# Normalising an attention output in its transposed form, with transfers that spread values and sums to dense rows

## The chip, the cores and the metric

One NeuronCore of a Trainium2 chip runs the whole kernel. The metric is device time in microseconds (us), the median of several executions.

## The reference, cut to what matters

Input x is (16, 256, 256): 16 sequences of 256 tokens with 256 features, all in float32. For each sequence:

```python
h   = sln(x, cond)                     # LayerNorm, then a gamma and a beta that depend on cond
qkv = (h @ Wqkv.T + bqkv)              # split into 16 heads of 16 features
att = softmax(q @ k.T) / 16            # per head, 256 x 256
out = (att @ v)                        # per head, back to (256, 256)
h1  = out @ Wp.T + bp + x
y   = sln(h1, cond) + h1
```

## The kernel before, in words

The kernel is one software pipeline over the 16 sequences (B = 16). In step b, sequence b has its scores exponentiated and weighed with V, sequence b+1 has its row maxima taken, b+2 its Q and K projected, b+3 its x normalised and transposed, b-1 its attention output projected, and b-2 its residual and second LayerNorm. A step has 16 slots, one for each head h. No scheduler places anything: the order of every engine is written out by hand, slot by slot, in a `step(b)` function per engine, and semaphores tie the engines together.

In each slot TensorE (`step`, L1253) does two matmuls of scores (`scores`, into `st_ps`, which ScalarE exponentiates, L602) and two of scores for the maxima (`scores_max`, L1010, into `sa_ps`, which VectorE reduces, `maximum`, L692). `sa_ps` has two banks, so `scores_max` of slot h waits for the reduce of slot h-2 (L1017). The projections are spread over the slots in quarters: `Q_SLOTS`, `K_SLOTS`, `V_SLOTS`, `P_SLOTS` (L45). All matmuls of one source line L976 (`mm`).

The part around the change is the way from P.V to the output projection, by two groups g of eight heads:

- `weigh` (L1038): P.V, transposed. Four heads at a time lie in 32-partition bands of `pv_ps[g]`; 16 partitions hold values, the other 16 the softmax sum, since V is stored beside 16 columns of ones (`v_st`, memset L475, written by ScalarE at L540). Group 0 runs in slot 10 of step b, group 1 in slot 2 of step b+1 (`PV_SLOTS`).
- `evict_out` (L544): ScalarE copies the 128x512 bank to `oT` in slots 12 (`S_O0`) and 3 (`S_O1`).
- `out_by_token` (L1058): TensorE turns it back with four 128x128 transposes (L1065), in slots 14 and 6.
- `normalise` (L704): VectorE takes reciprocals of 128x16 sums (L711, slots 15 and 7) and multiplies 128x256 values into `att` (L715, slots 15 and 8).
- `turn_att` (L1141): four more transposes (L1146) in slot 10.
- ScalarE makes the rounded high part `aT_h` (L575, slot 11), VectorE the low part `aT_l` (`low_att`, L773, L777, slot 11), and TensorE multiplies with `Wp` in slots 12 to 15 (`project_out`, L1002).

VectorE's order is the dictionary `between` (L857). A key (h, 0) stands ahead of the reduce of slot h, (h, 1) behind it. The statistics of x (`norm1`, L732: bn_stats L739, bn_aggr L745, variance L749) stand for sequence b+3 in slots 4 and 5. `residual` (L780) stands in slots 3, 4, 9 and 11, `low_qk` (L719, L727) in 5 and 7.

GpSimd (`step`, L417) does `rstd` and `norm_x` in slot 5, `add_beta` in 6, `maxima` (two small transfers of the row maxima, L368) in 3 and 11, `low_h` in 12. SyncE's queue issues in order (`step`, L308): eight transfers for group 1 of sequence b+1 (`stack`, L297), the load of x for b+4 (L314), eight for group 0 of b+2, then `gb` (L328) and the output (L332). The last sequence has an order of its own (`last_step` L1189, `finish` L1224, and VectorE's list from L930).

Of the kernel before, what the change touches and what calls it, by code (L numbers as in the profile page):

```python
# [45 lines left out]
S_MT1, S_AT, S_MT0, S_XT = 1, 10, 9, 10  # L46
# [8 lines left out]
S_OT1, S_OT0 = 6, 14  # L55


def cond_block(nc, x, condT, vectors, WgT, WbT, WqkvT, WpT, bp, out):
    gb_dram = nc.dram_tensor("gb_rows", (B, 2 * D), F32, kind="Internal").ap()
    with ExitStack() as ctx:  # L60
# [55 lines left out]
        rec = sb("rec", [P, 2, TT, HH, 1])  # L116
        att = sb("att", [P, TT, D])
# [86 lines left out]
        o_done = sem("o_done")  # L204
        rec_ready = sem("rec_ready")
        att_ready = sem("att_ready")
        attT_done = sem("attT_done")
# [5 lines left out]
        aT0_done = sem("aT0_done")  # L213
# [59 lines left out]
        def _(sp):  # L273
# [81 lines left out]
        def _(pool):  # L355
# [54 lines left out]

            def low_full(a, t, ready):
# [5 lines left out]
            def step(b):  # L417
                for h in range(H):
# [56 lines left out]
            pool.memset(v_st[:, :, :, :, HD:VC].rearrange("p a t h d -> p (a t h) d"), D ** 0.5).then_inc(v_ones_ready, 1)  # L475
# [10 lines left out]
            add_beta(B - 3)  # L486
            add_beta(B - 2)
# [8 lines left out]
        def _(act):  # L496
# [39 lines left out]
            def high_v(a, ps):  # L536
# [3 lines left out]
                nc.scalar.activation(v_st[:, par(a), :, :, 0:HD],  # L540
# [3 lines left out]
            def evict_out(a, g):  # L544
# [4 lines left out]
                wait(act, o_done, 2 * (a - 1) + g + 1)  # L549
# [123 lines left out]
            wait(act, o_done, 2 * B - 2)  # L673
# [3 lines left out]
            act.wait_ge(aT0_done, 1)  # L677
            wait(act, proj_done, B - 1)
            nc.scalar.activation(aT_h[:, 0, :], sa_ps[1][:, 0:N], ACT.Copy).then_inc(aTth_ready, 1)
# [4 lines left out]
        def _(dve):  # L684
# [19 lines left out]
            def normalise(a, g, stage):  # L704
# [27 lines left out]
            def norm1(a, stage):  # L732
# [8 lines left out]
                if stage == 1:  # L741
                    wait(dve, v_step, 3 * a + 1)
                    dve.memset(pause[:], 0.0)
# [28 lines left out]

            def low_att(a):  # L773
                if not has(a):
                    return
                wait(dve, aTh_ready, 1 * a + 1)
                dve.tensor_tensor(aT_l[:].rearrange("p k n -> p (k n)"), pv_ps[1][:],  # L777
                                  aT_h[:].rearrange("p k n -> p (k n)"), ALU.subtract).then_inc(aTl_ready, 1)
# [42 lines left out]
            def last_out(a, g):  # L821

                wait(dve, pv_done, 2 * a + g + 1)
                wait(dve, o_done, 2 * (a - 1) + g + 1)
                dve.tensor_copy(oT[:, g, :], pv_ps[g][:]).then_inc(oT_ready, 1)

            def last_high_att(a):

                wait(dve, attT_done, 1 * a + 1)
                wait(dve, proj_done, 1 * (a - 1) + 1)  # L830
                dve.tensor_copy(aT_h[:].rearrange("p k n -> p (k n)"), pv_ps[1][:]).then_inc(aTh_ready, 1)

            def low_att_half(k):

                bank = (sa_ps[1], pv_ps[1])[k]
                wait(dve, aTth_ready, k + 1)
                dve.tensor_tensor(aT_l[:, k, :], bank[:, 0:N], aT_h[:, k, :], ALU.subtract).then_inc(aTtl_ready, 1)

            def normalise_half(c):
# [14 lines left out]
            def step(b):  # L854
# [13 lines left out]
                    (11, 0): [lambda: low_max(b + 1, 0), lambda: low_att(b - 1), lambda: residual(b - 2, 5)],  # L868
                    (15, 0): [lambda: normalise(b, 0, 0)],
# [514 lines left out]
```

## Time and profile before

| what | value |
|---|---|
| median of 3 runs | 347.57 us (345.4 to 347.86) |
| the profiled execution's own time | 345.56 us |
| its span, first to last instruction | 343.8 us |
| TensorE busy, of the span | 97% |
| VectorE busy | 87% |
| ScalarE busy | 71% |
| GpSimd busy | 46% |
| granted TensorE clock, mean | 1.000 of full speed |

Busy shares say how long an engine had an instruction under way. TensorE's matmuls are pipelined and their ends modelled, so its 97% says that it is hardly ever without work, not that it runs at its peak. Durations of neighbouring VectorE instructions overlap by some 0.08 us, so what one costs in a full queue is the distance from its start to the start of the next.

### The profile page before, as it was taken

The page shows a single profiled execution, that of the slowest core. Times are in us where ns is not written, and L with a number is a line of the kernel's source. Part 1 is how long each engine was busy: PE and PEld are TensorE (multiplying, and loading weights), DVE is VectorE, ACT ScalarE, POOL GpSimd, SP SyncE. Part 2 cuts the span into 40 slices and gives each one's busy share as a digit, 9 for nine tenths or more (in the row PEclk, how much of TensorE's full clock was granted, in tenths as well). Part 3 has the DMA queues.
Part 4 walks back from the last instruction along what each step waited for, and adds up shares of the span by engine and source line. Part 5 has one row for each costly group of instructions (what it writes and reads, how often), then busy time and mean ns, then how long its engine had stood idle before and what let it go on. Part 6 is the DMA issues. An engine that isn't in the chain of part 4 may idle for free.

```text
span 343.8 us, 8981 instructions
## 1 busy us (share of the span) xinstructions
PE 332.5 (97%) x3173; PEld 286.8 (83%) x3173; DVE 298.3 (87%) x728; ACT 242.8 (71%) x476; POOL 159.1 (46%) x187
## 2 busy tenths in 40 slices
PE   8888999999999999999999999999999999999993
PEld 4677879888888988888888988888898988888773
DVE  4888978799898989899898989989898988999684
ACT  7664876868676786868686876868687786766740
POOL 5765544437164545527264644617254643224330
PEclk9999999999999999999999999999999999999999
DMA  7396445456555454555545454655556354652021
GB/s 242 126 218 186 124 115 140 129 155 157 170 141 156 134 152 135 173 156 170 142 125 169 134 155 134 184 142 160 161 135 157 98 157 123 182 146 67 16 61 61
DMA packets 47705, 48.87 MB, mean 142 GB/s; under 512 B 6287, under 2 KB 41374, under 8 KB 47662
## 3 DMA queue, kind: packets, MB, share of 16 engines
q1 hardware_dynamic: 44494, 46.74, 49.2%
q10 hardware_dynamic: 1184, 1.07, 1.2%
q0 software_dynamic: 1984, 0.51, 0.8%
q8 instruction: 25, 0.41, 0.5%
q14 instruction: 18, 0.15, 0.1%
HBM read 9.99 MB, written 4.23 MB: 41 GB/s over the span
## 4 chain that ended last, share of the span: by engine, by line
PE 87%; DVE 5%; DMA 3%; ACT 1%; issue 1%; ACTq 1%; SPq 0%; DVEq 0%
PE m L976 24%; PE st L976 19%; PE sa L976 18%; PE pv L976 17%; PE pv L1065 4%; DVE mx L692 3%; PE pv L1146 2%; PE m L1105 2%; DMA wqkv<-WqkvT_dram 2%; DMA kst<-qk_l 1%; PE pv L1079 1%; PE m L1079 1%; ACT p L602 0%; DVE qk_l L727 0%; ACTq L625 0%
## 5 line engine op out<-in xcount | busy, mean ns | idle before, releaser
L692 DVE TENSOR_REDUCE mx<-sa 128x2 f32<-128x512 f32 x256 | 171.5, 684 | 28.4 <-PE sa L976 27.3
L602 ACT ACTIVATE p<-st 128x512 f32<-128x512 f32 x240 | 140.9, 598 | 37.5 <-PE st L976 33.2
L976 PE MATMUL sa<-kst,qst 126*128 126x256 f32 x512 | 105.6, 288 | 2.0 <-DMA kst<-qk_l 1.0
L976 PE MATMUL st<-qst,kst 128*128 128x256 f32 x496 | 104.1, 292 | 0.2
L976 PEld LDWEIGHTS st<-qst,kst 128*128 128x128 f32 x496 | 75.1, 188 | 13.8 <-issue 12.8
L976 PEld LDWEIGHTS sa<-kst,qst 126*128 126x128 f32 x512 | 78.6, 189 | 4.6 <-DVE mx L692 1.7
L368 POOL DMA_DIRECT2D qst<-m_h x31 | 17.6, 567 | 112.4 <-DVE m_l L701 112.4
L976 PE MATMUL pv<-p,v_st 128*32 128x256 f32 x1008 | 61.0, 382 | 0.0
L976 PEld LDWEIGHTS pv<-p,v_st 128*32 128x32 f32 x1008 | 29.5, 109 | 21.0 <-ACT p L602 1.5
L976 PE MATMUL m<-hT_h,wqkv_h 128*128 128x256 f32 x128 | 36.8, 300 | 1.3 <-ACT hT_h L616 0.7
L377 POOL TENSOR_SCALAR xn<-xa,mv,rstd 128x256 f32<-128x256 f32 x28 | 34.2, 1227 | 1.5
L976 PE MATMUL m<-hT_h,wqkv_l 128*128 128x256 f32 x128 | 34.4, 280 | 0.4 <-DVE wqkv_l L915 0.4
L976 PE MATMUL m<-hT_l,wqkv_h 128*128 128x256 f32 x128 | 34.3, 279 | 0.0
L429 POOL TENSOR_TENSOR rstd<-vare,minus_half 128x4 f32<-128x4 f32 (+1 forms) x15 | 14.2, 948 | 41.0 <-DVE vare L749 37.0
L550 ACT ACTIVATE oT<-pv 128x512 f32<-128x512 f32 x29 | 17.2, 595 | 21.6 <-PE pv L976 21.6
L727 DVE SCALAR_TENSOR_TENSOR qk_l<-m,vecs,qk_h 128x256 fp32r<-128x256 f32 x60 | 25.9, 474 | 0.5 <-ACT qk_h L522 0.5
L976 PEld LDWEIGHTS m<-hT_h,wqkv_h 128*128 128x128 f32 x128 | 23.5, 189 | 2.2 <-issue 1.1
L976 PEld LDWEIGHTS m<-hT_h,wqkv_l 128*128 128x128 f32 x128 | 23.6, 190 | 0.6 <-DVE wqkv_l L915 0.6
L976 PEld LDWEIGHTS m<-hT_l,wqkv_h 128*128 128x128 f32 x128 | 23.4, 188 | 0.0
L395 POOL TENSOR_TENSOR h1b<-h,gb 128x512 f32<-128x512 f32 x15 | 19.4, 1291 | 6.9 <-DVE h L788 6.9
L386 POOL TENSOR_TENSOR xa<-xa,bias_b 128x512 f32<-128x512 f32 x16 | 20.6, 1289 | 0.0
L409 POOL TENSOR_TENSOR hT_l<-hT,hT_h 128x512 fp32r<-128x512 f32 x14 | 18.0, 1288 | 5.2 <-ACT hT_h L503 5.2
(149 smaller groups left out, 566.2 us busy)
## 6 DMA issues: line engine op xcount, KB each, us to landing
qst<-qk_h SPq DMA_DIRECT2D x64, 128.0 KB, 2.4
qst<-qk_l SPq DMA_DIRECT2D x64, 128.0 KB, 2.5
kst<-qk_h SPq DMA_DIRECT2D x62, 128.0 KB, 2.5
kst<-qk_l SPq DMA_DIRECT2D x62, 128.0 KB, 2.8
xa<-x_dram SPq DMA_DIRECT2D x16, 256.0 KB, 3.0
gb<-gb_rows SPq DMA_DIRECT2D x16, 256.0 KB, 3.9
out_dram<-y SPq DMA_DIRECT2D x15, 256.0 KB, 3.4
wqkv<-WqkvT_dram SPq DMA_DIRECT2D x1, 512.0 KB, 5.6
```

Source lines behind the costliest of these rows:

```text
L368: pool.dma_start(raw(qst[MAX_ROW + r:MAX_ROW + 1 + r, p, g * HH:(g + 1) * HH, :]) .rearrange("a h (t n) -> a (h t) n", t=TT), raw(m[:, g, ...
L377: o = pool.tensor_scalar(xn[:, t, :], xbuf(a)[:, t, :], mv[:, t, 0:1], rstd[:, 0, t:t + 1], ALU.subtract, ALU.mult)
L386: pool.tensor_tensor(xbuf(a), xbuf(a), bias_b[:].rearrange("p (a n) -> p a n", a=1).broadcast_to([P, TT, D]), ALU.add).then_inc(xdb_ready, 1)
L395: pool.tensor_tensor(h1b[:], h1[:], gb[:, par(a), D:2 * D].rearrange("p (a n) -> p a n", a=1) .broadcast_to([P, TT, D]), ALU.add).then_inc ...
L409: pool.tensor_tensor(hT_l[:, par(a)], hT[:], hT_h[:, par(a)], ALU.subtract).then_inc(hTl_ready, 1)
L429: pool.tensor_tensor(rstd[:, which], vare[:, which], minus_half[:, which], ALU.pow).then_inc(rstd_ready, 1)
L550: nc.scalar.activation(oT[:, g, :], pv_ps[g][:], ACT.Copy).then_inc(oT_ready, 1)
L602: nc.scalar.activation(p32[:, h, :], st_ps[h % 2][:], ACT.Exp).then_inc(exp_done, 1)
L692: dve.tensor_reduce(mx[:, par(a), h // HH, (h % HH) * TT:(h % HH + 1) * TT], sa_ps[h % 2][:].rearrange("p (t n) -> p t n", t=TT), AX.X, AL ...
L727: o = dve.scalar_tensor_tensor(out=qk_l[:, par(a), t, g, :], in0=ps[:, g * N:(g + 1) * N], scalar=vecs[:, 4 + t, g:g + 1], in1=qk_h[:, par ...
L976: return nc.tensor.matmul(o, l, r, start=start, stop=stop)
L1065: o = nc.tensor.transpose(pv_ps[g][:, t * N + c * P:t * N + (c + 1) * P], oT[:, g, c * N + t * P:c * N + (t + 1) * P], ident[:])
```

## The change

V and the ones are interleaved, so that P.V leaves a value on each even partition and its sum on the odd one beside it. The 128x512 copy `oT` is then sent by two transfers of 128 KB per group: the 64 even partitions to `o_rows[:, g, :]` (128 partitions x 256) and the 64 odd ones to `o_sums[:, g, :]`. VectorE takes the reciprocal of `o_sums` (128x256, in place) and multiplies `o_rows` by it, in place. `o_rows` is now the transposed attention output, with its rows in an order that the host puts into `WpT` and the V bias. `out_by_token` and `turn_att` are gone. `aT_h` is made from `o_rows` in slot 10, `aT_l` by GpSimd instead of VectorE. The statistics of x move from slots 4 and 5 (for b+3) to 12 to 14 (for b+4).

```diff
-S_MT1, S_AT, S_MT0, S_XT = 1, 10, 9, 10
+S_MT1, S_AH, S_MT0, S_XT = 1, 10, 9, 10
-S_OT1, S_OT0 = 6, 14
...
+            def send_out(a, g):
+                if not has(a):
+                    return
+                sp.wait_ge(oT_ready, 2 * a + g + 1)
+                wait(sp, aTh_ready, 1 * a)
+                wait(sp, aTl_ready, 1 * a)
+                for n, dst in enumerate((o_rows, o_sums)):
+                    sp.dma_start(dst[:, g, :], oT[n:P:2, g, :]).then_inc(o_in[g], 16)
...
                     sp.dma_start(xbuf(b + 4), x_t[b + 4]).then_inc(x_in[(b + 4) % 4], 16)
+                send_out(b - 1, 1)
                 if has(b):
                     stack(b + 2, 0)
...
+                send_out(b, 0)
                 if has(b - 2):
                     wait(sp, y_ready, 1 * (b - 2) + 1)
...
+            def low_att(a):
+                wait(pool, aTh_ready, 1 * a + 1)
+                pool.tensor_tensor(aT_l[:], o_rows[:], aT_h[:], ALU.subtract).then_inc(aTl_ready, 1)
...
+                    if h == 10 and has(b - 1):
+                        low_att(b - 1)
                     if h == 11 and has(b):
                         maxima(b + 1, 0)
...
-                    if h == S_AT + 1 and has(b - 1):
-                        wait(act, attT_done, 1 * (b - 1) + 1)
+                    if h == S_AH and has(b - 1):
+                        wait(act, att_ready, 2 * (b - 1) + 2)
                         wait(act, proj_done, 1 * (b - 2) + 1)
-                        nc.scalar.activation(aT_h[:].rearrange("p k n -> p (k n)"), pv_ps[1][:],
-                                             ACT.Copy).then_inc(aTh_ready, 1)
+                        nc.scalar.activation(aT_h[:].rearrange("p k n -> p (k n)"),
+                                             o_rows[:].rearrange("p k n -> p (k n)"), ACT.Copy).then_inc(aTh_ready, 1)
...
-                sums = pv_ps[g][:].rearrange("p (t h d) -> p t h d", t=TT, h=HH)
                 if stage == 0:
-                    wait(dve, o_done, 2 * a + g + 1)
-                    dve.reciprocal(rec[:, g], sums[:, :, :, HD:HD + 1]).then_inc(rec_ready, 1)
+                    wait(dve, o_in[g], 32 * (a + 1))
+                    dve.reciprocal(o_sums[:, g, :], o_sums[:, g, :]).then_inc(rec_ready, 1)
                 if stage == 1:
                     wait(dve, rec_ready, 2 * a + g + 1)
-                    wait(dve, attT_done, 1 * (a - 1) + 1)
-                    dve.tensor_tensor(att[:, :, g * P:(g + 1) * P].rearrange("p t (h d) -> p t h d", h=HH),
-                                      sums[:, :, :, 0:HD], rec[:, g].broadcast_to([P, TT, HH, HD]),
+                    dve.tensor_tensor(o_rows[:, g, :], o_rows[:, g, :], o_sums[:, g, :],
                                       ALU.mult).then_inc(att_ready, 1)
...
-                    (2, 1): [lambda: low_max(b, 1)],
-                    (3, 0): [lambda: residual(b - 2, 0), lambda: residual(b - 2, 1)],
-                    (4, 0): [lambda: residual(b - 2, 2), lambda: norm1(b + 3, 0)],
-                    (4, 1): [lambda: residual(b - 2, 3), lambda: norm1(b + 3, 1)],
-                    (5, 0): [lambda: norm1(b + 3, 2)],
+                    (2, 1): [lambda: low_max(b, 1), lambda: normalise(b - 1, 0, 0)],
+                    (3, 0): [lambda: residual(b - 2, 0), lambda: normalise(b - 1, 0, 1), lambda: residual(b - 2, 1)],
+                    (4, 0): [lambda: residual(b - 2, 2)],
+                    (4, 1): [lambda: residual(b - 2, 3)],
...
-                    (11, 0): [lambda: low_max(b + 1, 0), lambda: low_att(b - 1), lambda: residual(b - 2, 5)],
-                    (15, 0): [lambda: normalise(b, 0, 0)],
-                    (15, 1): [lambda: normalise(b, 0, 1)],
+                    (12, 1): [lambda: norm1(b + 4, 0)],
+                    (13, 1): [lambda: norm1(b + 4, 1)],
+                    (14, 1): [lambda: norm1(b + 4, 2)],
+                    (11, 0): [lambda: low_max(b + 1, 0), lambda: residual(b - 2, 5)],
...
             low_max(B - 1, 1)
             for stage in (1, 2, 3):
                 residual(B - 3, stage)
+            normalise(B - 2, 0, 0)
+            normalise(B - 2, 0, 1)
             last_out(B - 2, 1)
+            residual(B - 3, 4)
             normalise(B - 2, 1, 0)
             normalise(B - 2, 1, 1)
             last_high_att(B - 2)
-            low_att(B - 2)
-            residual(B - 3, 4)
             last_out(B - 1, 0)
```

For the last sequence, the second group of heads keeps the old way (`normalise_half`, two transposes), with strides changed for the interleaved layout.

## Rows read from the trace of the kernel before

**Rows 1.** The page: busy time, and the chain that ended last

```profile
PE 332.5 (97%) x3173; PEld 286.8 (83%) x3173; DVE 298.3 (87%) x728; ACT 242.8 (71%) x476; POOL 159.1 (46%) x187
...
PE 87%; DVE 5%; DMA 3%; ACT 1%; issue 1%; ACTq 1%; SPq 0%; DVEq 0%
```

**Rows 2.** Busy time by engine in stretches of one step each

```profile
core 0: us, PE busy (x) PEld busy (x) DVE busy (x) ACT busy (x) POOL busy (x), PEclk, DMA share, GB/s
73.02:92.50 19.48, 19.48 (x197) 17.28 (x196) 17.82 (x45) 14.55 (x30) 9.38 (x10) 1.00 0.55 150
...
170.45:189.94 19.49, 19.49 (x196) 17.29 (x195) 17.84 (x44) 14.58 (x30) 9.38 (x10) 1.00 0.54 153
...
267.90:287.40 19.50, 19.50 (x197) 17.29 (x196) 17.85 (x44) 14.57 (x30) 9.36 (x10) 1.00 0.53 145
```

**Rows 3.** The chain in order of time, one step: start, us, what

```profile
173.62 0.44 PE pv L1065 x4
...
178.37 0.44 PE pv L1146 x4
178.80 1.86 PE pv L976 x32
183.51 0.44 PE pv L1065 x4
```

**Rows 4.** Timeline of VectorE in that step: start, us, instruction, [idle before]

```profile
174.87 0.25 DVE L711 RECIPROCAL rec<-pv 128x16 f32<-128x16 f32 x1
175.04 0.62 DVE L692 TENSOR_REDUCE mx<-sa 128x2 f32<-128x512 f32 x1
...
176.36 0.41 DVE L715 TENSOR_TENSOR att<-pv,rec 128x256 f32<-128x256 f32 x1
176.69 1.28 DVE L692 TENSOR_REDUCE mx<-sa 128x2 f32<-128x512 f32 x2
...
179.47 0.69 DVE L777 TENSOR_TENSOR aT_l<-pv,aT_h 128x512 fp32r<-128x512 f32 x1
180.08 0.87 DVE L816 SCALAR_TENSOR_TENSOR y<-y,rstd,h1b 128x256 f32<-128x256 f32 x2
181.38 1.98 DVE L692 TENSOR_REDUCE mx<-sa 128x2 f32<-128x512 f32 x3 [0.43 <-PE sa L976]
183.54 0.69 DVE L692 TENSOR_REDUCE mx<-sa 128x2 f32<-128x512 f32 x1 [0.18 <-PE sa L976]
...
187.40 0.69 DVE L692 TENSOR_REDUCE mx<-sa 128x2 f32<-128x512 f32 x1 [0.24 <-PE sa L976]
```

**Rows 5.** Groups of instructions with shapes kept apart: VectorE, small ones and multiplies

```profile
L711 DVE RECIPROCAL rec<-pv 128x16 f32<-128x16 f32 x31 | 7.7, 248 | 0.9 <-PE pv L1065 0.9
...
L843 DVE RECIPROCAL rec<-sa 128x8 f32<-128x8 f32 x1 | 0.2, 208 | 0.4 <-PE sa L1232 0.4
...
L843 DVE RECIPROCAL rec<-pv 128x8 f32<-128x8 f32 x1 | 0.2, 199 | 0.0
...
L893 DVE COPY vecs<-pv 128x14 f32<-128x14 f32 x1 | 0.2, 165 | 0.0
```

**Rows 6.** The same view: two float32 multiplies from PSUM, 256 and 128 columns

```profile
L715 DVE TENSOR_TENSOR att<-pv,rec 128x256 f32<-128x256 f32 x31 | 12.8, 414 | 0.1
...
L845 DVE TENSOR_TENSOR att<-pv,rec 128x128 f32<-128x128 f32 x1 | 0.3, 291 | 0.0
```

**Rows 7.** SyncE's queue in that step, and its line L297: us to landing

```profile
170.64 0.54 SPq L314 DMA_DIRECT2D xa<-x_dram  x1
174.69 1.17 SPq L297 DMA_DIRECT2D qst<-qk_h  x2
```

```profile
DMA to landing us min/median/max: 2.3/2.5/4.5
```

**Rows 8.** The last step: VectorE's timeline

```profile
322.36 0.69 DVE L825 COPY oT<-pv 128x512 f32<-128x512 f32 x1 [0.55 <-PE pv L976]
...
326.10 0.69 DVE L777 TENSOR_TENSOR aT_l<-pv,aT_h 128x512 fp32r<-128x512 f32 x1
```

**Rows 9.** The last step: the chain in order of time

```profile
328.59 1.41 PE m L976 x12
330.00 0.44 PE pv L1065 x4
```

**Rows 10.** Groups: one low part as GpSimd makes it

```profile
L409 POOL TENSOR_TENSOR hT_l<-hT,hT_h 128x512 fp32r<-128x512 f32 x14 | 18.0, 1288 | 5.2 <-ACT hT_h L503 5.2
```

**Rows 11.** Who waited for whom: us in total, times, longest us

```profile
PEld sa L976 <- DVE mx L692: 1.7, 5, 0.6
```

More of the change, by code:

```diff
@@ L115, in cond_block @@
         oT = sb("oT", [P, 2, 2 * N])
-        rec = sb("rec", [P, 2, TT, HH, 1])
-        att = sb("att", [P, TT, D])
+        rec = sb("rec", [P, TT, HH, 1])
+        o_rows = sb("o_rows", [P, 2, N])
+        o_sums, att = wg, wqkv[:, :, 0:D]
         aT_h = sb("aT_h", [P, KT, N], F32R)
@@ L486, in _ @@
             add_beta(B - 3)
+            low_att(B - 2)
             add_beta(B - 2)
@@ L548, in evict_out @@
                 wait(act, pv_done, 2 * a + g + 1)
-                wait(act, o_done, 2 * (a - 1) + g + 1)
+                wait(act, o_in[g], 32 * a)
                 nc.scalar.activation(oT[:, g, :], pv_ps[g][:], ACT.Copy).then_inc(oT_ready, 1)
@@ L672, in _ @@
             act.wait_ge(pvt_done, 1)
-            wait(act, o_done, 2 * B - 2)
+            wait(act, o_in[1], 32 * (B - 1))
             nc.scalar.activation(oT[:, 1, 0:N], pv_ps[1][:, 0:N], ACT.Copy).then_inc(oTt_ready, 1)
@@ L676, in _ @@
             nc.scalar.activation(oT[:, 1, N:2 * N], m0[:, 0:N], ACT.Copy).then_inc(oTt_ready, 1)
-            act.wait_ge(aT0_done, 1)
+            wait(act, att_ready, 2 * B - 1)
             wait(act, proj_done, B - 1)
-            nc.scalar.activation(aT_h[:, 0, :], sa_ps[1][:, 0:N], ACT.Copy).then_inc(aTth_ready, 1)
+            nc.scalar.activation(aT_h[:, 0, :], o_rows[:, 0, :], ACT.Copy).then_inc(aTth_ready, 1)
             act.wait_ge(aT1_done, 1)
@@ L742, in norm1 @@
                     wait(dve, v_step, 3 * a + 1)
+                    wait(dve, xn_ready, 1 * a)
                     dve.memset(pause[:], 0.0)
@@ L771, in low_h_direct @@
                 dve.tensor_tensor(hT_l[:, par(a)], hT[:], hT_h[:, par(a)], ALU.subtract).then_inc(hTl_ready, 1)
[L773 to L778, printed above, removed]
             def residual(a, stage):
@@ L823, in last_out @@
                 wait(dve, pv_done, 2 * a + g + 1)
-                wait(dve, o_done, 2 * (a - 1) + g + 1)
+                wait(dve, o_in[g], 32 * a)
                 dve.tensor_copy(oT[:, g, :], pv_ps[g][:]).then_inc(oT_ready, 1)
             def last_high_att(a):
-                wait(dve, attT_done, 1 * a + 1)
+                wait(dve, att_ready, 2 * a + 2)
                 wait(dve, proj_done, 1 * (a - 1) + 1)
-                dve.tensor_copy(aT_h[:].rearrange("p k n -> p (k n)"), pv_ps[1][:]).then_inc(aTh_ready, 1)
+                dve.tensor_copy(aT_h[:], o_rows[:]).then_inc(aTh_ready, 1)
             def low_att_half(k):
-                bank = (sa_ps[1], pv_ps[1])[k]
+                whole = (o_rows[:, 0, :], pv_ps[1][:, 0:N])[k]
                 wait(dve, aTth_ready, k + 1)
-                dve.tensor_tensor(aT_l[:, k, :], bank[:, 0:N], aT_h[:, k, :], ALU.subtract).then_inc(aTtl_ready, 1)
+                dve.tensor_tensor(aT_l[:, k, :], whole, aT_h[:, k, :], ALU.subtract).then_inc(aTtl_ready, 1)
             def normalise_half(c):
@@ L874, in step @@
                 if first(b + 1):
-                    for slot in ((4, 0), (4, 1), (5, 0), (5, 1), (7, 1), (11, 0)):
+                    for slot in ((4, 0), (4, 1), (5, 1), (7, 1), (11, 0)):
                         del between[slot]
@@ L942, in _ @@
             residual(B - 2, 0)
+            for stage in (1, 2, 3):
+                residual(B - 2, stage)
             normalise(B - 1, 0, 0)
             normalise(B - 1, 0, 1)
-            for stage in (1, 2, 3):
-                residual(B - 2, stage)
             normalise_half(0)
@@ L1041, in weigh @@
                 wait(pe, exp_done, 16 * b + HH * (g + 1))
-                wait(pe, att_ready, 2 * b + g - 1)
+                wait(pe, oT_ready, 2 * b + g - 1)
                 if g == 0:
@@ L1047, in weigh @@
                     pe.wait_ge((v_ones_ready, bias_ready)[g], 1)
-                if g == 1:
-                    wait(pe, aTl_ready, 1 * b)
                 for q in range(2):
@@ L1056, in weigh @@
                 o.then_inc(pv_done, 1)
-            def out_by_token(a, g):
-                if not has(a):
-                    return
-                wait(pe, oT_ready, 2 * a + g + 1)
-                for t in range(TT):
-                    for c in range(2):
-                        o = nc.tensor.transpose(pv_ps[g][:, t * N + c * P:t * N + (c + 1) * P],
-                                                oT[:, g, c * N + t * P:c * N + (t + 1) * P], ident[:])
-                o.then_inc(o_done, 1)
             def warm_up(n):
@@ L1139, in project_second @@
                 o.then_inc(q_done, 1)
-            def turn_att(a):
-                wait(pe, att_ready, 2 * a + 2)
-                for t in range(TT):
-                    for k in range(KT):
-                        o = nc.tensor.transpose(pv_ps[1][:, k * N + t * P:k * N + (t + 1) * P],
-                                                att[:, t, k * P:(k + 1) * P], ident[:])
-                o.then_inc(attT_done, 1)
             def last_scores(h):
@@ L1170, in last_weigh @@
                 if half == 0:
-                    wait(pe, aTl_ready, B - 1)
+                    wait(pe, oT_ready, 2 * (B - 2) + 2)
                 else:
@@ L1191, in last_step @@
                 last_scores(1)
-                wait(pe, att_ready, 2 * (B - 2) + 1)
+                wait(pe, oT_ready, 2 * (B - 2) + 1)
                 transpose_max(B - 1, 1, pv_ps[0])
@@ L1224, in finish @@
             def finish():
-                wait(pe, att_ready, 2 * B - 1)
-                for t in range(TT):
-                    o = nc.tensor.transpose(sa_ps[1][:, t * P:(t + 1) * P], att[:, t, 0:P], ident[:])
-                o.then_inc(aT0_done, 1)
+                wait(pe, oT_ready, 2 * B - 1)
                 for c, bank in ((0, sa_ps[0]), (1, pv_ps[0])):
@@ L1265, in step @@
                         turn_x(b + 3)
-                    if h == S_AT and has(b - 1):
-                        turn_att(b - 1)
                     for g in range(2):
@@ L1271, in step @@
                             weigh(a, g)
-                    if h == S_OT1:
-                        out_by_token(b - 1, 1)
-                    if h == S_OT0:
-                        out_by_token(b, 0)
                     if h == (0 if first(b) else S_MT1) and has(b):
-                        wait(pe, att_ready, 2 * (b - 1) + 1)
+                        wait(pe, oT_ready, 2 * (b - 1) + 1)
                         if first(b):
@@ L1364, in by_kind, with by_rows @@
                                w[:, :, 2].reshape((D,) + w.shape[3:])])
+    def by_rows(w):
+        return np.moveaxis(w.reshape((2, 2, HH // 2, HD) + w.shape[1:]), 1, 3).reshape(w.shape)
+    bqkv = by_kind(get("bqkv"))
     arrays = {
@@ L1374 @@
         "WqkvT": by_kind(get("Wqkv")).T,
-        "WpT": get("Wp").T, "bp": get("bp"),
+        "WpT": by_rows(get("Wp").T), "bp": get("bp"),
     }
```

19 lines of the change are left out of this document (7 added, 12 removed).

## The prediction

> **What bounds the kernel now.** I read the page's busy shares first, then its chain, then stretches of one step. TensorE is busy 97% of the span and has 87% of the chain [rows 1]. The stretches say it more sharply: from 73.02 to 287.40 us eleven steps in a row last 19.5 us each, and in each TensorE is busy for all of it, while VectorE is busy for 17.8 to 17.9 us (the first, one in the middle and the last of them: [rows 2]). So TensorE has no slack at all in the steady part, and VectorE has 19.49 - 17.84 = 1.65 us a step. That second number matters as much as the first, because the change takes work off the one and, as I will argue, puts work on the other. The clock stands at its upper level (2.4 GHz, a granted share of 1.00) in every step [rows 2].
>
> **TensorE: what goes.** Each step loses three blocks of four transposes, at 0.44 us each in the chain [rows 3]: 1.32 us. TensorE's own work per step falls to 19.49 - 1.32 = 18.17 us. Nothing is added on it.
>
> **VectorE: what goes.** Costs are taken from start to start [rows 4]. The low part of 128x512: 180.08 - 179.47 = 0.61 us. Two multiplies from PSUM at 176.69 - 176.36 = 0.33 us: 0.66. Two reciprocals of 128x16: 0.17 us in the full queue (175.04 - 174.87); the second stands alone and counts 0.25, its duration [rows 4, 5]. Together 1.69 us.
>
> **VectorE: what comes.** Two multiplies of 128x256, both operands now in SBUF. The one there is now, with an operand in PSUM, has a slope of (414 - 291) / 128 = 0.96 ns a column [rows 6], one column a cycle or so, and the new one has as many columns: 0.33 us each, 0.66 for the two.
>
> Two reciprocals of 128x256. This is the number on which the whole case turns, for the trace has none longer than 16 columns. What it has: 248 ns at 16 columns (31 of them) and 199 and 208 ns at 8 [rows 5]. The difference is 40 to 49 ns for 8 columns, 5.0 to 6.1 ns a column, where the multiply's slope would give 8 ns. A second way: a copy of 14 columns takes 165 ns [rows 5], of which some 150 are fixed if it goes at a column a nanosecond; then the reciprocals' rest is 98 ns for 16 and 49 to 58 for 8, 6 to 7 ns a column. A third: in the full queue one costs 0.17 us against about 0.07 us that a multiply costs over its columns (0.33 - 0.26), so 0.10 us for 16 columns. All three say some 6 ns a column. The strides can't explain that away wholly: the small reciprocals read one element in 32, but the multiply's 16-wide runs of the same bank pay nothing for the gaps. So I take 0.07 + 256 x 6.1 ns = 1.63 us in the queue for one. Bounds: below, 256 columns at the multiply's slope, 0.33 us, if the small ones' price is something fixed or due to single-element reads; above, 7 ns a column and 0.07, 1.86 us.
>
> VectorE then has 17.84 - 1.69 + 0.66 + 2 x 1.63 = 20.07 us of work in a step. That is more than the 19.49 us a step takes now, and more than TensorE's 18.17: the bound changes engine. VectorE still can't run without gaps, since a reduce waits for its scores. Before, it idles 0.43, 0.18 and 0.24 us ahead of bare slots [rows 4]; in slots 15, 0 and 1 of the new order it again has a reduce alone (0.61 us, half of a pair that lies without a gap, against a slot of over 0.8), and once more it catches up while TensorE weighs for 1.86 us in slot 10 [rows 3]. I add 0.6 us (0.2 for each of two or three slots and the rest there). A step of 20.65 us, then: 1.16 us more than now. TensorE stands still in it at slots 5, 9 and 10, where `scores_max` needs a bank that the reduce behind a long reciprocal or a `low_qk` has not yet freed.
>
> The Trainium skill ("VectorE: DVE Perf Modes", First, the fixed hardware budget) says that reciprocal runs on an iterative divide with a repeat count of 8. Read as eight cycles of 0.96 GHz a column, an estimate from that page, the long reciprocal takes 2.2 us and the step 21.8. By that rule the small ones would differ by 67 ns; the trace has 40 to 49 [rows 5] and doesn't agree in size, though it does in kind. Another page ("Vector Engine (DVE) Microarchitecture Reference", Measured stream behaviour on trn2) has built-in one-source operations at 1.0417 ns a column and 75 ns fixed: 0.34 us for the long one. The trace speaks against it by the same rows. Both are rivals below.
>
> **Moved and hidden parts.** The statistics of x cost VectorE the same in slots 12 to 14 as in 4 and 5; there they use slots that had little, which is why I add 0.6 us of idle and not the old 1.65. The x they need was loaded 8 slots earlier. ScalarE: the same copies, one read from SBUF and a slot earlier; it has 19.49 - 14.58 = 4.9 us of slack a step [rows 2], so nothing. Both interleaved strides (V and its ones) I take at nothing for the same cover. GpSimd: one more low part, 1.29 us [rows 10], on an engine busy 9.4 of 19.5 us [rows 2]; it stands ahead of the maxima's two transfers and `low_h`. `aT_h` can be ready in slot 10, before VectorE's row maxima of slot 11, so it is done by about the time the maxima can go: nothing; without that cover, a late first score in the next step, up to 1.3 us.
>
> **The transfers.** SyncE issues four more a step, each at 0.59 us (1.17 for two) [rows 7]. Those for group 1 stand behind eight stacks and the load of x, which is issued at 170.64; two more would be out by about 172.4 and land by 171.8 + 2.5 = 174.3, at worst 176.3 with 4.5 us [rows 7]. VectorE wants them at its slot 7, at 174.87 before [rows 4], and some 0.5 us later in the new step because a reciprocal and a multiply stand in slots 2 and 3. Behind that wait queues everything of VectorE, the reduce of slot 7 first, and so TensorE. Median landing gives 1 us of margin: nothing. The next stacks go at 174.69, after the two. Group 0's transfers have half a step. Bound above: 1 us a step.
>
> **The last step** has no reduces, but its order is a chain. The old one: copy at 322.36, transposes, reciprocal, multiply, turn, high part, low part ending at 326.79 [rows 8], projection from 328.59 [rows 9]. The new one puts a reciprocal and a multiply ahead of the copy (1.96, less 0.55 that VectorE idled there: copy at 323.8, done 324.5), then two issues and a landing (0.6 + 2.5: 327.6), reciprocal and multiply (1.96: 329.5), high part (0.7), low part on GpSimd (1.3): 331.5, against a projection at 328.59 now: 2.9 us late. Behind it another long reciprocal and multiply in place of short ones (1.96 for 0.6) stand on VectorE ahead of the last half, and 0.44 us of transposes at 330.00 go [rows 9]. I take +4 us, bounds 0 and 6.
>
> **The sum.** Sequences 0 to 13 pass the two normalisations inside 14 full steps: 14 x 1.16 = 16.2 us. Plus 4 at the end, less 0.44 for one block in step 0. From the profiled execution's 345.56 us: 365.3. The median of the runs shown is 347.57, 2.0 above; they spread by 2.5 us, so I give 365.
>
> **Rivals.**
> 1. *The long reciprocal streams at a column a cycle* (0.33 us). For: the trace has no long one, and the small ones read single elements. Against: the slope of rows 5. VectorE has 17.84 - 1.69 + 0.66 + 0.67 = 17.5 us, TensorE bounds at 18.2: 14 x 1.3 = 18 us saved, the end about even: 328. This is the case of the other side. The point from which it decides: VectorE's load plus idle equals 19.49 us at (19.49 - 0.6 - 16.81) / 2 = 1.04 us for one reciprocal, 3.8 ns a column. Below that the change is faster.
> 2. *The long reciprocal costs more than any reading of the short ones gives*, a column at twice the rows' lower slope of 4 or 5 ns, 2.2 us: 16.81 + 4.4 + 0.6 = 21.8 us a step, 14 x 2.3 + 5 = 37: 383. Against: rows 5 as said.
> 3. *The transfers come late*, because more of them share the engines or wait for the queue: 0.7 us a step on top, 10 us: 375. For: landings up to 4.5 us. Against: 1 us of margin.
> 4. *Something between* (3.5 to 4.5 ns a column): 342 to 354.
>
> **How the numbers follow.** Forecast 0.68, rival 1 0.14, rival 2 0.05, rival 3 0.07, rival 4 0.06. The forecast's own spread: 5.0 ns a column gives 1.35 us, a step of 20.1 and, with a shorter end, 357; 7 ns 1.86 us, 21.1 and 373. The range is 352 to 378: it leaves out rival 1 and 2. A measurement here can tell about 1% from no change. Faster by over 1%: rival 1 and a part of 4, 0.15; within 1%: 0.04; slower: 0.81.
>
> **What would show it.** Right: reciprocals of 128x256 at 1.5 to 1.8 us; VectorE over 95% busy in the steady part and first in the chain; TensorE waiting for the reduce (5 times and 1.7 us in all now [rows 11], then 2 us a step); steps near 20.6 us. Wrong: reciprocals of 0.4 us, with steps of 18.2 us and TensorE still without a gap; or VectorE idle ahead of its slot-7 reciprocal, released by a transfer.

## The result, and the profile after

The changed kernel takes 373.04 us (median of 4 runs, 372.62 to 376.89) against 347.54 us for the kernel before: a ratio of 1.077, 95% interval 1.069 to 1.086. Ratios, here and below, are of mean times, and leave out an execution more than 1.5% above the fastest of its kernel (one, in e3_apart). The forecast was 365 us, slower, with a range of 352 to 378. The profiled execution took 373.01 us, with a span of 371.2 us against 343.8.

The page of the changed kernel, busy shares and chain, the answer to [rows 1]:

```profile
PE 333.8 (90%) x2987; PEld 273.2 (74%) x2987; DVE 341.0 (92%) x713; ACT 245.6 (66%) x476; POOL 179.1 (48%) x202
...
PE 43%; DVE 38%; issue 13%; DMA 2%; ACT 1%; ACTq 1%; DVEq 0%; POOL 0%; SPq 0%
```

TensorE has 186 matmul records fewer, and yet the kernel is longer: its part of the chain went from 87% to 43%, and VectorE's from 5% to 38%. One step, in the busy times by stretch, the answer to [rows 2]:

```profile
core 0: us, PE busy (x) PEld busy (x) DVE busy (x) ACT busy (x) POOL busy (x), PEclk, DMA share, GB/s
160.54:181.45 20.91, 19.37 (x184) 16.23 (x183) 20.50 (x44) 14.74 (x30) 10.65 (x11) 1.00 0.59 169
181.45:202.36 20.91, 19.36 (x184) 16.20 (x183) 20.52 (x45) 14.77 (x30) 10.65 (x11) 1.00 0.57 163
```

A step lasts 20.91 us instead of 19.49 (forecast: 20.65). VectorE is busy for 20.5 of it (98%). Groups of the page that carry this, the first the answer to [rows 5]:

```profile
L728 DVE RECIPROCAL wg<-wg 128x256 f32<-128x256 f32 x31 | 53.7, 1733 | 1.9 <-DMA wg<-oT 1.9
...
L817 DVE SCALAR_TENSOR_TENSOR y<-h,mv,gb 128x256 f32<-128x256 f32 x30 | 24.5, 856 | 0.0
```

The long reciprocal takes 1733 ns (`o_sums` lies in the old tile `wg`). Against 248 ns at 16 columns that is 1485 / 240 = 6.2 ns a column, as the short ones had said. Behind it, VectorE's queue goes on 1.66 us after its start. The second row is one that I had not forecast; it comes back below.

The chain in order of time shows how a step hangs together (start, us, what):

```profile
184.24 0.67 DVE mx L710
184.90 1.66 DVE wg L728
...
188.21 0.69 DVE mx L710
188.90 0.04 issue
188.95 0.51 PE sa L986 x2
189.46 0.44 PE m L1102 x4
189.90 1.86 PE pv L986 x32
...
198.35 0.07 DVE mx L710
198.42 0.54 issue
198.96 0.27 DVE m_l L719
199.23 1.66 DVE wg L728
```

It isn't VectorE all round. From slot 2 (198.35) to the reduce of slot 8 (188.21 + 20.91 + 0.69 = 209.81) the step runs on VectorE, 11.5 us; there `scores_max` of slot 10 takes over, and up to the next slot 2 it runs on TensorE, 9.4 us. Who waited for whom confirms the place:

```profile
PEld sa L986 <- DVE mx L710: 29.0, 49, 1.4
```

That was 1.7 us in 5 times before [rows 11]; now it is some 2 us a step. In TensorE's timeline of one step these waits stand at slots 5, 9 and 10, the three that were forecast:

```profile
182.17 0.51 PE L986 MATMUL sa<-kst,qst 126*128 126x256 f32 x2 [0.43 <-DVE mx L710]
187.16 0.50 PE L986 MATMUL sa<-kst,qst 126*128 126x256 f32 x2 [0.37 <-DVE mx L710]
188.95 0.51 PE L986 MATMUL sa<-kst,qst 126*128 126x256 f32 x2 [0.42 <-DVE mx L710]
```

To see where the 27.4 us of span went, I take the start of the residual's bn_stats, once a step, as a mark. From the first to the twelfth mark the kernel before goes from 71.91 to 286.56 us and the changed one from 76.16 to 306.11: 15.3 us in 11 steps. Ahead of the first mark lie 4.25 us (two such steps make 2.8 of them; beside them the stretch from 30 to 40 us has a clock share of 0.83, against 1.00 before), in the step after the twelfth 1.6, in the last steps 6.2 (4.1 from mark 14 to 15 and 2.2 behind it).

**The end.** TensorE's timeline there (start, us, instruction, [idle before]), and the busy times of the stretch:

```profile
352.79 0.58 PE L986 MATMUL m<-wp_h,aT_h 128*128 128x256 f32 x1 [3.52 <-POOL aT_l L424]
353.17 0.41 PE L986 MATMUL m<-wp_h,aT_l 128*128 128x256 f32 x1
```

```profile
core 0: us, PE busy (x) PEld busy (x) DVE busy (x) ACT busy (x) POOL busy (x), PEclk, DMA share, GB/s
350.00:355.00 5.00, 2.21 (x10) 2.21 (x11) 3.35 (x6) 0.67 (x2) 1.27 (x1) 0.61 0.21 59
```

TensorE stood still for 3.52 us until GpSimd had the low part. Then the clock granted was the lower level, 1.2 GHz, for a part of the stretch (PEclk 0.61 over the whole), so that twelve matmuls that took 1.41 us before [rows 9] took 2.94. The wait I had forecast at 2.9 us; the 1.5 us of clock I had not.

### The profile page after: what moved, and what is told of

Same layout as the page of the kernel before. It is cut to its first block, busy times and chain, and to the rows that moved or that the text cites. A ratio compares the mean times of both kernels' runs of the same rounds, so it can differ in the third digit from the quotient of the medians.

```text
span 371.2 us, 8687 instructions
## 1 busy us (share of the span) xinstructions
PE 333.8 (90%) x2987; PEld 273.2 (74%) x2987; DVE 341.0 (92%) x713; ACT 245.6 (66%) x476; POOL 179.1 (48%) x202
## 4 chain that ended last, share of the span: by engine, by line
PE 43%; DVE 38%; issue 13%; DMA 2%; ACT 1%; ACTq 1%; DVEq 0%; POOL 0%; SPq 0%
DVE wg L728 14%; PE sa L986 13%; PE m L986 11%; PE st L986 9%; DVE mx L710 8%; PE pv L986 7%; DVE qk_l L742 5%; DVE stats L802 3%; DVE h L797 2%; PE m L1102 2%; DVE o_rows L731 1%; DVE m_l L719 1%; DMA kst<-qk_l 1%; DVE mv L808 1%; DVE y L817 1%
## 5 line engine op out<-in xcount | busy, mean ns | idle before, releaser
L710 DVE TENSOR_REDUCE mx<-sa 128x2 f32<-128x512 f32 x256 | 168.7, 672 | 14.1 <-PE sa L986 10.8
L986 PE MATMUL sa<-kst,qst 126*128 126x256 f32 x512 | 111.6, 300 | 19.9 <-DVE mx L710 18.7
L986 PEld LDWEIGHTS st<-qst,kst 128*128 128x128 f32 x496 | 76.5, 191 | 14.5 <-issue 12.4
L986 PE MATMUL pv<-p,v_st 128*32 128x256 f32 x1008 | 61.9, 386 | 0.0
L728 DVE RECIPROCAL wg<-wg 128x256 f32<-128x256 f32 x31 | 53.7, 1733 | 1.9 <-DMA wg<-oT 1.9
L986 PE MATMUL m<-hT_h,wqkv_h 128*128 128x256 f32 x128 | 36.0, 294 | 1.2 <-ACT hT_h L634 0.7
L424 POOL TENSOR_TENSOR aT_l<-o_rows,aT_h 128x512 fp32r<-128x512 f32 x15 | 19.4, 1292 | 31.9 <-ACT aT_h L593 25.6
L986 PEld LDWEIGHTS m<-hT_h,wqkv_h 128*128 128x128 f32 x128 | 23.7, 191 | 2.2 <-issue 2.2
L817 DVE SCALAR_TENSOR_TENSOR y<-h,mv,gb 128x256 f32<-128x256 f32 x30 | 24.5, 856 | 0.0
L986 PEld LDWEIGHTS m<-hT_l,wqkv_h 128*128 128x128 f32 x128 | 23.7, 190 | 0.0
```

The lines of the kernel that those rows point to most:

```text
L424: pool.tensor_tensor(aT_l[:], o_rows[:], aT_h[:], ALU.subtract).then_inc(aTl_ready, 1)
L710: dve.tensor_reduce(mx[:, par(a), h // HH, (h % HH) * TT:(h % HH + 1) * TT], sa_ps[h % 2][:].rearrange("p (t n) -> p t n", t=TT), AX.X, AL ...
L728: dve.reciprocal(o_sums[:, g, :], o_sums[:, g, :]).then_inc(rec_ready, 1)
L817: o = dve.scalar_tensor_tensor(out=y[:, par(a), t, :], in0=h1[:, t, :], scalar=mv2[:, t, 0:1], in1=gb[:, par(a), 0:D], op0=ALU.subtract, o ...
L986: return nc.tensor.matmul(o, l, r, start=start, stop=stop)
```

## The experiments

**b1_stats: the statistics of x alone.** In the kernel before:

```diff
+                    wait(dve, xn_ready, 1 * a)
...
-(4, 0): [lambda: residual(b - 2, 2), lambda: norm1(b + 3, 0)],
-(4, 1): [lambda: residual(b - 2, 3), lambda: norm1(b + 3, 1)],
-(5, 0): [lambda: norm1(b + 3, 2)],
+(4, 0): [lambda: residual(b - 2, 2)],
+(4, 1): [lambda: residual(b - 2, 3)],
+(12, 1): [lambda: norm1(b + 4, 0)],
+(13, 1): [lambda: norm1(b + 4, 1)],
+(14, 1): [lambda: norm1(b + 4, 2)],
```

> The kernel before with only the statistics of x moved to slots 12 to 14, for b+4. Theory: TensorE bounds, VectorE has 1.65 us a step to spare, so no change: within 0.3% of the kernel before. Rival (the move costs or saves by itself): over 0.5% either way.

Measured: 345.76 against 345.40 us, ratio 1.0005 (0.998 to 1.003). No change: the move costs nothing in the kernel before.

**b2_recips: the long reciprocals alone.** In the kernel before:

```diff
+            def spare(a, g):
+                if not has(a):
+                    return
+                dve.reciprocal(wb[:, g, :], wg[:, g, :])
...
-(2, 1): [lambda: low_max(b, 1)],
+(2, 1): [lambda: low_max(b, 1), lambda: spare(b - 1, 0)],
-(7, 0): [lambda: normalise(b - 1, 1, 0)],
+(7, 0): [lambda: normalise(b - 1, 1, 0), lambda: spare(b - 1, 1)],
```

> The kernel before with two reciprocals of 128x256 added to VectorE's list of each step, behind the low part of the maxima in slot 2 and behind the short reciprocal in slot 7; nobody reads what they write. Theory (the long reciprocals alone make VectorE the bound): 17.8 + 2 x 1.66 + some 0.4 us of idle, steps of 21.3 to 21.7 us, 371 to 378 us. Rival (the rest of the change, transfers and waits, makes most of the loss): steps under 20.3 us, below 360 us.

Measured: 381.58 us against 345.31, ratio 1.105 (1.100 to 1.111), steps of 22.33 us. The rival falls, and the time lies above the expected 371 to 378 us. Two instructions that nobody reads cost more than the whole change, which had taken other work off VectorE. The step is 0.6 us longer than the upper end of what load and idle gave. VectorE is busy for 20.96 us of it, near the load I had added up, and idle for 1.37 where I had taken some 0.4.

**e1_stream and e2_half: the reciprocal shortened.**

e1_stream inverts no sum, e2_half only half of the columns. First the edit of e1_stream, then that of e2_half:

```diff
-dve.reciprocal(o_sums[:, g, :], o_sums[:, g, :]).then_inc(rec_ready, 1)
+dve.tensor_tensor(o_sums[:, g, :], o_sums[:, g, :], o_sums[:, g, :],
+                  ALU.mult).then_inc(rec_ready, 1)
```

```diff
-dve.reciprocal(o_sums[:, g, :], o_sums[:, g, :]).then_inc(rec_ready, 1)
+dve.reciprocal(o_sums[:, g, 0:P], o_sums[:, g, 0:P]).then_inc(rec_ready, 1)
```

> The long reciprocal is replaced by a multiply of the same 128x256 tile with itself, in place (so the sums are not inverted; everything else stands). Theory (VectorE's load, made by the two long reciprocals, bounds the step): VectorE loses 2 x (1.66 - 0.33) = 2.7 us of work a step, TensorE bounds again without its transposes, steps of about 18.3 us, 330 us in all, some 5% faster than the kernel before. Rival (the transfers or the new waits bound it): still above 360 us.

> The long reciprocal runs over 128 of its 256 columns (half of the sums are not inverted). Theory: 6.4 ns a column, so 0.90 us instead of 1.73; VectorE's work falls by 2 x 0.83 us a step; steps of 19.2 to 19.4 us, 347 to 350 us: within 1% of the kernel before, which is near the break-even that I put at 1.04 us. Rival (a large fixed cost): a reciprocal of 1.2 us or more and over 355 us.

Measured: e2_half 359.38 us, ratio 1.040 (1.035 to 1.046), most steps 19.9 to 20.0 us (three of the first eleven 20.2 to 20.9; VectorE waited 8 times for a transfer, 6.7 us in all). e1_stream 349.14 us, ratio 1.008 (1.005 to 1.012), steps of 19.4 to 19.8 us. The reciprocal of 128 columns:

```profile
L728 DVE RECIPROCAL wg<-wg x31: 929/931/954, 53.9 to 345.0; 128x128 f32<-128x128 f32 x31
```

(min, median and max in ns.) Three lengths now: 248 ns at 16 columns, 931 at 128, 1733 at 256: 6.1 and 6.3 ns a column. That part of both expectations holds. The times don't: I had put break-even at 1.04 us for one reciprocal, and even a stand-in of 0.33 us only comes to about even. TensorE's work of some 18.2 us a step doesn't come through, so something else holds the step at 19.5. VectorE's timeline in e1_stream, ahead of slot 7:

```profile
195.32 0.43 DVE L728 TENSOR_TENSOR wg<-wg 128x256 f32<-128x256 f32 x1 [0.59 <-DMA wg<-oT]
```

There are nine such waits in the run, 5.7 us in all.

**e9_stream_xload: the transfer two thirds of a microsecond earlier.** In e1_stream, SyncE's queue:

```diff
+                send_out(b - 1, 1)
                 if has(b + 4) and has(b):
...
                     sp.dma_start(xbuf(b + 4), x_t[b + 4]).then_inc(x_in[(b + 4) % 4], 16)
-                send_out(b - 1, 1)
```

> e1_stream with the load of x issued behind the pair of transfers instead of ahead of it. Theory (with a short reciprocal, the transfer that slot 7 waits for holds the step): the pair goes out 0.55 us earlier, VectorE's wait of 0.6 us ahead of slot 7 goes, steps of 18.9 to 19.3 us instead of 19.5, 338 to 344 us. Rival (VectorE's order in slots 3 to 8 holds it): steps of 19.4 us or more.

Measured: 347.17 us, ratio 1.004 (1.001 to 1.008), beside e1_stream's 1.008: little. One of the seven waits in the steady steps is left (0.88 us; with three near the end 3.8 us in all), and the steps are still 19.5 us. What took the wait's place stands in the timelines of VectorE and of GpSimd:

```profile
195.50 0.87 DVE L743 SCALAR_TENSOR_TENSOR qk_l<-m,vecs,qk_h 128x256 fp32r<-128x256 f32 x2
196.28 1.33 DVE L732 TENSOR_TENSOR o_rows<-o_rows,wg 128x256 f32<-128x256 f32 x1
197.54 1.27 DVE L710 TENSOR_REDUCE mx<-sa 128x2 f32<-128x512 f32 x2
```

```profile
196.04 1.29 POOL L405 TENSOR_TENSOR h1b<-h,gb 128x512 f32<-128x512 f32 x1
```

The multiply takes 1.33 us where its median is 0.416. It starts 0.24 us after the start of a GpSimd instruction that ends at 197.33, and is done 0.28 us after that end. Both its operands lie in SBUF. The multiply that it replaces read PSUM and never took over 425 ns.

The same GpSimd instruction stands there in e1_stream. GpSimd, then VectorE:

```profile
196.10 1.29 POOL L405 TENSOR_TENSOR h1b<-h,gb 128x512 f32<-128x512 f32 x1
```

```profile
197.60 1.28 DVE L710 TENSOR_REDUCE mx<-sa 128x2 f32<-128x512 f32 x2
```

It ends at 197.39 there and at 197.33 here, and the reduces of slot 8, for which TensorE waits in both runs, start at 197.60 and 197.54. So the wait for the transfer was hidden behind the collision, and taking it away gained nothing here. No run has a short reciprocal with neither of the two and nothing in their place, so what the step would be then isn't shown.

**e3_apart: the same collision in the changed kernel.** There it hits y's first part, which is the odd row of the page above. The timelines of VectorE and GpSimd in the changed kernel:

```profile
189.41 1.73 DVE L817 SCALAR_TENSOR_TENSOR y<-h,mv,gb 128x256 f32<-128x256 f32 x2
191.07 0.68 DVE L710 TENSOR_REDUCE mx<-sa 128x2 f32<-128x512 f32 x1
```

```profile
189.19 1.28 POOL L424 TENSOR_TENSOR aT_l<-o_rows,aT_h 128x512 fp32r<-128x512 f32 x1 [1.18 <-ACT aT_h L593]
```

The pair took 0.87 us before. GpSimd's low part is what the change put there. The experiment moves the pair from behind the reduce of slot 9 to ahead of that of slot 11:

```diff
-(9, 1): [lambda: residual(b - 2, 4)],
-(11, 0): [lambda: low_max(b + 1, 0), lambda: residual(b - 2, 5)],
+(11, 0): [lambda: low_max(b + 1, 0), lambda: residual(b - 2, 4), lambda: residual(b - 2, 5)],
```

> VectorE's y = (h1 - mean) * gb (residual stage 4) moves from behind the reduce of slot 9 to ahead of that of slot 11, so that it no longer starts while GpSimd makes the attention's low part. Theory (the instruction with two SBUF inputs waits for the whole of the GpSimd instruction): its longest falls from 1.5 to under 0.6 us in the steady steps, a step gets 0.5 to 0.9 us shorter, 7 to 12 us in all: 361 to 366 us. Rival (the 1.5 us come from gb's transfer or from a semaphore): no change, 373 us.

VectorE's timeline in e3_apart:

```profile
190.27 0.27 DVE L719 SCALAR_TENSOR_TENSOR m_l<-m,m_h 16x128 fp32r<-16x128 f32 x1
190.47 0.86 DVE L817 SCALAR_TENSOR_TENSOR y<-h,mv,gb 128x256 f32<-128x256 f32 x2
...
192.64 1.29 DVE L710 TENSOR_REDUCE mx<-sa 128x2 f32<-128x512 f32 x2 [0.40 <-PE sa L985]
```

The mechanism holds: 0.86 us for the pair again. Its price doesn't: the steps shrink by 0.17 us only (20.74), while TensorE is weighing at that place and VectorE now waits for scores (0.40 us, the last line). Over all, 377.19 us (374.98 to 380.94), ratio 1.087 (1.080 to 1.093), against the changed kernel's 1.077 (1.069 to 1.086): not faster, and hardly to be told from it. In its profile, one step of 23.56 us (a transfer that took 4.75 us to land, then the lower clock) and a last part of 17.7 us instead of 15.4 took more than the steady steps gave. I can't say whether the order provokes these. A late transfer at the same place, some 264 us into the run, stands in the profiles of e4_lowdve and e6_tail too (4.35 and 4.75 us to land, steps of 23.1 and 23.4 us), and not in those of the changed kernel and of e10_order; its cause is open.

**e4_lowdve: the low part on VectorE again.**

```diff
-                    if h == 10 and has(b - 1):
-                        low_att(b - 1)
...
-(11, 0): [lambda: low_max(b + 1, 0), lambda: residual(b - 2, 5)],
+(11, 0): [lambda: low_max(b + 1, 0), lambda: low_att(b - 1), lambda: residual(b - 2, 5)],
```

> The changed kernel with the attention's low part on VectorE again (slot 11), not on GpSimd. Theory (VectorE has room behind slot 9, where TensorE weighs, so neither the collision nor the low part costs there): steps within 0.2 us of 20.9, and the last step 0.5 to 1.5 us shorter, since VectorE makes the low part in 0.6 us where GpSimd takes 1.3: 370 to 373 us. Rival (VectorE's total load decides, whatever the slot): 0.3 us a step or more either way, over 4 us.

Measured: 372.70 us, ratio 1.078 (1.071 to 1.085), steps of 20.75 us, but for two of 22.6 and 23.1 us in which a transfer came late. From mark 14 to 15 it takes 13.7 us instead of 14.7. The steady steps and the end are as expected: behind slot 9 VectorE has room for 0.6 us of work, or for a collision. That the total fell into the expected range is in part chance, for the two long steps cost 4.2 us that the expectation didn't have.

This run is also the plainest test of the collision. y's pair stands where it stood in the changed kernel, and only GpSimd's instruction is gone:

```profile
189.21 0.87 DVE L816 SCALAR_TENSOR_TENSOR y<-h,mv,gb 128x256 f32<-128x256 f32 x2
```

None of the 30 takes over 479 ns, where the longest was 1501. That leaves nothing to `gb`'s transfer or to a semaphore, the rival named for e3_apart.

**e5_double: more transfers.** Each pair is preceded by two of the same size:

```diff
-                for n, dst in enumerate((o_rows, o_sums)):
-                    sp.dma_start(dst[:, g, :], oT[n:P:2, g, :]).then_inc(o_in[g], 16)
+                for n, dst in enumerate((wb, wqkv[:, :, D:2 * D], o_rows, o_sums)):
+                    sp.dma_start(dst[:, g, :], oT[n % 2:P:2, g, :]).then_inc(o_in[g], 16)
...
```

> The changed kernel with each pair of transfers preceded by two more of the same size, to tiles that nobody reads (1.2 us of issue and 256 KB more per group). Theory: the pair has 1 to 1.3 us of margin at slot 7, so up to 0.3 us a step more, 373 to 378 us. Rival (the transfers are what costs): 1 us a step or more, over 385 us.

Measured: 416.27 us, ratio 1.206 (1.197 to 1.214), steps of 23.7 us. The expectation is far off. VectorE ahead of slot 7:

```profile
201.54 1.75 DVE L728 RECIPROCAL wg<-wg 128x256 f32<-128x256 f32 x1 [1.76 <-DMA wg<-oT]
```

Two issues of 0.62 us delay the pair by 1.25 us, and VectorE waits for 1.76. So more than the margin of 1 us is used up: the chain has SyncE's stacks of the next step behind the pair of group 0, so that pair pushes the other back as well. Until the reduce behind that reciprocal TensorE stands still for 2.23 us, and then the chain in order of time reads:

```profile
206.40 0.85 PE m L1102 x4
207.25 2.72 PE pv L986 x32
```

In the changed kernel these take 0.44 and 1.86 us. The clock share of such a step is 0.93 instead of 1.00. So of the 2.8 us a step, some 1.3 are the lower clock behind the wait. Two more pairs on SyncE's queue a step are more than this order has room for.

**e8_actq and e7_stream_actq: the transfers from ScalarE's queue.** Behind the copy to `oT`, in the changed kernel and in e1_stream:

```diff
                 nc.scalar.activation(oT[:, g, :], pv_ps[g][:], ACT.Copy).then_inc(oT_ready, 1)
+                act.wait_ge(oT_ready, 2 * a + g + 1)
...
+                for n, dst in enumerate((o_rows, o_sums)):
+                    act.dma_start(dst[:, g, :], oT[n:P:2, g, :]).then_inc(o_in[g], 16)
```

> The streaming stand-in for the reciprocal as in e1_stream, and the transfers of values and sums issued by ScalarE right behind its copy, instead of SyncE behind eight stacks and the load of x. Theory (once the reciprocal is short, the step is held by the transfer that slot 7 waits for, 0.6 to 1.3 us where VectorE waits): no wait ahead of that instruction, steps of 18.3 to 18.9 us instead of 19.5, 333 to 340 us. Rival (VectorE's load in slots 3 to 8 alone makes the 19.5 us): steps stay at 19.4 us or more, 345 us and over.

> The changed kernel with its long reciprocals, and the transfers issued by ScalarE as in e7_stream_actq. Theory (with a long reciprocal VectorE comes to slot 7 later than the transfer): no change in the steady steps, 20.9 us, 371 to 374 us. Rival (late transfers cost in the changed kernel too): over 3 us faster.

Measured: e7_stream_actq 368.43 us, ratio 1.065 (1.059 to 1.071), steps of 20.7 us; e8_actq 390.21 us, ratio 1.127 (1.121 to 1.133), steps of 21.97 us. Both expectations fail, upwards. The chain of e7_stream_actq:

```profile
200.63 0.61 ACT oT L570
201.24 0.02 issue
201.26 0.54 ACTq L575
201.80 0.03 issue
201.83 0.63 ACTq L575
202.46 0.05 issue
202.51 0.60 ACT p L627
```

The waits for transfers are gone from the steady steps (three at the end are left), but the two issues stand in ScalarE's own order, ahead of the exponential of slot 3, for which TensorE waits. ScalarE has 5 us of slack a step and none in this place. These runs don't decide between transfer and load in e1_stream. e9_stream_xload shows that the transfer alone doesn't hold it.

**e6_tail: the last step's order.**

```diff
+            last_out(B - 2, 1)
             normalise(B - 2, 0, 0)
             normalise(B - 2, 0, 1)
-            last_out(B - 2, 1)
             residual(B - 3, 4)
```

> The changed kernel with only the last step's order changed: the copy of P.V goes ahead of group 0's reciprocal and multiply, which then run while the transfer is on its way. Theory: the projection of the last but one sequence starts about 2 us earlier (it started 4.2 us behind the place it had in the kernel before, and the clock fell while TensorE waited): 1.5 to 3.5 us faster than the changed kernel, 369 to 371.5 us. Rival (the tail hangs on the scores, not on this chain): no change, 373 us.

Measured: 372.06 us (369.64 to 372.15), ratio 1.073 (1.068 to 1.079). TensorE's timeline:

```profile
351.62 0.39 PE L986 MATMUL m<-wp_h,aT_h 128*128 128x256 f32 x1 [1.55 <-POOL aT_l L424]
```

The wait is 1.55 us instead of 3.52, the clock share stays at 1.00 behind it, and from mark 14 to 15 it takes 11.5 us instead of 14.7. This profile also has one step of 23.4 us, in which the transfer came late, and the median of the runs moved by only 1 us. The chain is as described, but the median lies above the expected 369 to 371.5 us, and the gain over all isn't clear of the spread.

**e10_order: three orders together** (e3_apart, e6_tail, and the load of x behind the pair).

> The changed kernel with three changes of order: y's stage 4 in slot 11 (as e3_apart), the copy first in the last step (as e6_tail), and x's load behind the pair of transfers. Theory: steps of 20.75 us (2 us in all), a last step some 3 us shorter, and no step lengthened by a late transfer: 366 to 369 us, still some 6% over the kernel before. Rival: the orders undo each other, 371 us or more.

Measured: 373.05 us, ratio 1.079 (1.073 to 1.086). Expected were 366 to 369; the rival, 371 or more, came true. The steps are 20.74 us and none is lengthened, as expected, but what the end gains in one place it loses in another: its last full step took 18.9 us instead of 15.4, with a clock share of 0.93 over that stretch; the next took 11.6 instead of 14.7, with a transfer of 3.3 us in its chain. None of the orders tried gets back what the reciprocals cost.

## Why the prediction was right, and where it was not

- *The reciprocal at 6 ns a column*: right. 1.66 us in the queue against 1.63; 6.1 and 6.3 ns a column over three lengths. This term decided the sign: two such reciprocals alone make the kernel before 2.8 us a step slower (b2_recips), twice the loss of the change, and without them the changed kernel is back at 1.008 (e1_stream).
- *VectorE's work of 20.07 us, and 0.6 us of idle*: 20.5 busy and 0.4 idle. Of the 20.5, 0.8 is the collision with GpSimd that I didn't have; so the work proper was some 0.4 less than forecast. A likely reason is that a reduce counts 0.61 us in the full queue and 0.69 after a gap, and gaps became fewer; no run tests it. The step came out at 20.91 against 20.65, the 14 steps at 14 x 1.42 = 19.9 against 16.2 us. That it came so near is in part luck: the same sum falls short by 0.6 us in b2_recips, 0.8 in e2_half and 1.3 in e1_stream.
- *Where TensorE stands still, slots 5, 9 and 10, for some 2 us a step*: right. *VectorE first in the chain*: wrong. It has 38% against TensorE's 43%, since it binds only from slot 2 to slot 8.
- *Load plus idle as the step's length, with break-even at 1.04 us* (rival 1): wrong. It says what a step can't be shorter than, not what it is. Shortening the reciprocal to 0.87 and 0.33 us gave 19.95 and 19.5 us, not 19.1 and 18.2. With two banks of maxima, VectorE can lag TensorE by about a slot, so what counts in the changed kernel is its work from slot 2 to slot 8. The old room of 1.65 us a step lay outside most of that stretch: 0.43, 0.18 and 0.41 us ahead of slots 11, 14 and 15, some 0.5 ahead of slots 2 and 3, and none in slots 4 to 10. In the step shown of each of the two short runs (e1_stream, e9_stream_xload) what holds slot 8 is GpSimd's instruction and the collision with it, to which the sum had no term. With a reciprocal that streams, the change as built comes out about even (349.14 and 347.17 us), not at 328; what it would reach without the collision isn't shown.
- *Transfers at nothing, with 1 us of margin*: right for the changed kernel. The second of the pair is issued at 181.71, lands 2.2 us later by the median, and VectorE takes it at 184.83, 0.9 us behind; it waited once in the run, 1.9 us, in the last step. The margin is no more than VectorE's lateness: with a short reciprocal the wait is there (0.59 us), and one more pair for each group costs 2.8 us a step.
- *Moving the statistics, at nothing*: right (b1_stats).
- *GpSimd's low part, at nothing*: right in its own time, wrong in what it does to VectorE, though that costs little in this kernel (0.17 us a step), as TensorE is weighing meanwhile.
- *The last step, +4 us*: 6.2. The 2.9 us wait was there (3.5); the lower clock behind it, 1.5 us, was missing.
- *Nothing at the start but 0.44 us less*: wrong. Ahead of the first mark the run lost 1.4 us more than its two steps, in part at the lower clock. Steps (3.7), end (2.2) and start (1.8) all came out longer than forecast, which is why 373 lies near the upper end of the range.

The Trainium skill has the rule for the collision ("SBUF — State Buffer", Who interferes with whom): a VectorE instruction with two SBUF inputs and a GpSimd instruction that reads SBUF can't share the second read port, and the later one waits for the whole of the earlier. By that rule, the first of the pair at 189.41 waits to 190.47, then takes its 0.47: 1.53 us in all. The longest one measured is 1.501. The same working gives the multiply of e9_stream_xload 197.33 - 196.28 + 0.42 = 1.47 us, against 1.33. The trace agrees within 0.15 us, and the rule would have told which operands to watch: the old multiply had one in PSUM.

## What to carry to other kernels

Before an operation on a few compact values is turned into one on a full dense tile, look at its slope and not at its time: here 16 columns cost 0.25 us and 256 cost 1.73, and the sixteenfold repetition of each sum was paid in full. An engine's slack is worth something only in the slots in which it lies: take the work of the stretch between two points where the engines meet, not the step's total. And when operands move from PSUM to SBUF, check what GpSimd reads at that moment.

## What was not expected of the hardware

- An instruction of VectorE with both inputs in SBUF took 1.50 us instead of 0.47 (y) and 1.33 instead of 0.42 (multiply) when a GpSimd instruction of 1.28 us had started before it; without that instruction, and in the same place, 0.48 at most (e4_lowdve).
- An issue of a transfer takes ScalarE 0.54 to 0.63 us of its own order; with the four of a step there, of which one pair stands on the chain, the step was 1.05 us longer (e8_actq, 21.97 against 20.92).
- After TensorE had stood still for 3.52 us, its matmuls started 0.21 us apart instead of 0.12, for at least 2.5 us; after 1.55 us of standing still in e6_tail they started 0.12 apart. In e5_double it stood still for 2.23 us, and four transposes then took 0.85 us instead of 0.44.
